# Layer 1's queries, keys and values as three fp16 products of high and low halves, and a new table of tick places

## The chip, the cores and the metric

The kernel runs on one core of one Trainium2 chip. TensorE (PE) multiplies, VectorE (DVE), ScalarE (ACT) and GpSimd (POOL) work on elements, SyncE (SP) issues every transfer. The metric is the device time of one execution in microseconds, the median of the runs.

## What is computed

Four layers follow one another on a batch of 32 sequences of 256 tokens and 256 channels. Layer 0 is a conditioned block of two normalisations over the whole sequence and two 256x256 products. Layer 1 is attention of 16 heads with a bias and a mask, and an MLP. Layer 2 is a stencil. Layer 3 is causal attention and an MLP with a gate. The change touches the first lines of layer 1:

```python
emb = jax.nn.silu(_sin_emb(timestep)) @ W_ada + b_ada
scale, shift = jnp.split(emb[:, None, :], 2, axis=-1)
x = _ln(src) * (1.0 + scale) + shift
q = (x @ Wq + bq).reshape(B, S, N_HEAD, HEAD_DIM).transpose(0, 2, 1, 3)
k = (x @ Wk + bk).reshape(B, S, N_HEAD, HEAD_DIM).transpose(0, 2, 1, 3)
v = (x @ Wv + bv).reshape(B, S, N_HEAD, HEAD_DIM).transpose(0, 2, 1, 3)
scores = jnp.einsum('bhqd,bhkd->bhqk', q / math.sqrt(HEAD_DIM), k)
```

## The kernel before

One program is written out for all 32 batches. Layers 0 to 2 of batch b begin at tick 64 b, layer 3 at tick 64 b + 160, so that layer 1 of one batch runs beside layer 3 of one two or three batches earlier. Every piece of work has a name and a place (the tables `P`, `LATE`, `OWN`, `SPLIT`, and `place`); `OWN` holds the places of the first two batches (0, 1) and of the last two (-2, -1). For each engine the ticks are walked in order and the pieces due at a tick are written in the order in which the loop names them. A tick therefore is not a time: it only sets the order of pieces on one engine. Each engine works its list strictly in that order, and waits on semaphores where it needs another engine (`Lane.wait_ge`). SP has such a list too, of transfers.

The pieces around the change, in the order of the data of a batch:

- DVE `n1_*` and `n2_*`: the two normalisations of layer 0 (statistics L874 to L878, sum L883 to L885, `all_center` L890, `all_scale` L895 and L899, `all_gate` L903); PE's `n1_ones` (L1513) and `n2_ones` (L1531) spread the sums, POOL's `n1_rstd` and `n2_rstd` (L531, L533) make the reciprocal roots; PE's `win` and `wout` are the two products (`lin_T` L1332, `lin_N` L1395).
- POOL's `xb` (L574) adds a row of `rows` to X, DVE's `x1` adds the product and takes statistics (L909, L912), ACT's `x1_norm` and POOL's `ada` (L582, L584) normalise and modulate.
- PE's `t1` turns X into bank F (L1402), ACT's `t1_out` copies it to H1 (L1226). PE's `q1`, `k1` (L1332) and `v1` (L1395) multiply H1 by the weights in Wf in fp32. ACT's `q1_out` and `k1_out` add the bias (L1179) and write a rounded copy (L1194), POOL's `q1_lo` and `k1_lo` the remainder (L547, L550), DVE's `v1_out` fills VW (L1009).
- SP's `stack` (L475, L479) moves QU, QH, KU, KH into the stacks Qs and Ks. PE's `score` (L1426), DVE's `bias` (L931), ACT's `exp` (L1153), PE's `flip` (L1436), the copies `ev0` and `ev1` (L1158, L938), PE's `pv` (L1451) and `ct` (L1461) are a unit of attention: two heads; 8 units a batch and layer.
- Layer 3 makes the same three products from fp16 halves already: ACT's `t3_out` writes the high half HB (L1256), DVE's `t3_lo` the low half (`rest`, L870), PE's `split_T` (L1344) and `split_N` (L1357) make three products for each fp32 one from WS_p3. The MLPs' first products are made so as well; their weights are split once, at the start (`split_scale` L800 and others).
- `warm` and `keep` put filler matmuls (L1293) on PE at the places and in the numbers of the table `WARM`.

Of the kernel before, what the change touches and what calls it, by code (L numbers as in the profile page):

```python
# [48 lines left out]
def begin(layer, b):  # L49
# [15 lines left out]
    "s_pm": 67, "s_b": 68, "s_r": 75, "s_rp": 80, "s_re": 95, "s_ha": 81, "s_w": 98, "s_ab": 99, "s_row": 98,  # L65
    "s_mm": 102, "s_f": 101, "ld_w1": -24, "ld_sten": -46, "ld_w3": -277, "coefs": -21, "split_w1": -8,
    "split_w1_hi": -4, "split_w1_lo": -2, "split_p3": 46, "split_p3_hi": 50, "split_p3_lo": 54, "split_w3": 82,
    "split_w3_hi": 88, "split_w3_lo": 92, "film_a": -72, "film": -62, "adas": -57, "scr": -48, "m3": -58,
# [127 lines left out]
def build(nc, A, OUT, scr, NB=32):  # L196
# [11 lines left out]
    def at(t, piece):  # L208
        return due[piece].get(t, [])
# [1513 lines left out]
```

## Time and profile before

| what | us |
|---|---|
| median of 3 runs | 2625.06 (2623.78 to 2630.91) |
| the profiled execution | 2623.82 |
| its span, first to last instruction | 2622.5 |
| mean granted TensorE clock over the span | 0.993 |

| engine | busy us | share of the span |
|---|---|---|
| PE, matmuls | 2511.0 | 96% |
| PE, weight loads | 2045.2 | 78% |
| DVE | 2000.5 | 76% |
| ACT | 2104.4 | 80% |
| POOL | 1525.1 | 58% |

Matmuls are pipelined and overlap in the records, so the duration of one (0.273 us for an fp16 one of 256 columns) is not what it costs: the distance from one start to the next is. A matmul of fp32 stands as two records. Idle time is counted from 150 ns on.

### The profile page before, as it was taken

Reading aid. Unit: us, or ns where it says so; the run is one execution under the profiler, and the core shown is the slowest. Engines: PE = TensorE matmul, PEld = TensorE weight load, DVE = VectorE, ACT = ScalarE, POOL = GpSimd, SP = SyncE. Lnnn points to the kernel's source line nnn. Section 1 sums busy time; section 2 is a strip of 40 time slices with the busy share of each in tenths; the row PEclk is TensorE's granted clock in tenths of the full one; section 3 lists DMA queues with packets and bytes.
Section 4 is the critical chain, followed back from the end, with each engine's and each line's share of the span. In section 5 each row is a group of like instructions: output and inputs, shape, how many; then the busy total and the mean of one; then the engine's idle time right before and its main releaser. Section 6 shows DMA issues by size and latency. Waiting matters only on the chain.

```text
span 2622.5 us, 57389 instructions
## 1 busy us (share of the span) xinstructions
PE 2511.0 (96%) x18897; PEld 2045.2 (78%) x18897; DVE 2000.5 (76%) x7326; ACT 2104.4 (80%) x4691; POOL 1525.1 (58%) x1486
## 2 busy tenths in 40 slices
PE   7888999999999999999999999999999999999988
PEld 6666788887878888788788788787777788877776
DVE  6777787778887777888777787877788877778653
ACT  1557888888888888888888888988888888888775
POOL 3566666555666655656665565675556666555421
PEclk8899999999999999999999999999999999999999
DMA  5444344433344443334443333444333344333311
GB/s 207 122 131 114 99 118 127 120 109 97 97 113 120 125 114 113 91 97 121 123 123 112 102 104 97 121 125 119 108 103 94 110 121 127 116 103 96 84 29 33
DMA packets 178103, 287.64 MB, mean 110 GB/s; under 512 B 46032, under 2 KB 99280, under 8 KB 177424
## 3 DMA queue, kind: packets, MB, share of 16 engines
q1 hardware_dynamic: 177808, 283.97, 37.4%
q8 instruction: 153, 2.51, 0.4%
q14 instruction: 142, 1.16, 0.2%
HBM read 174.64 MB, written 8.45 MB: 70 GB/s over the span
## 4 chain that ended last, share of the span: by engine, by line
PE 48%; POOL 19%; DVE 12%; ACT 10%; issue 5%; SPq 3%; DMA 2%; POOLq 0%; DVEq 0%; ACTq 0%
PE bank L1413 12%; POOL BT L562 9%; PE bank L1344 7%; PE bank L1436 6%; PE bank L1395 5%; PE bank L1332 5%; PE bank L1451 4%; PE bank L1426 4%; DVE PB L931 3%; PE bank L1402 2%; PE bank L1584 2%; SPq L479 2%; ACT AA L1179 2%; ACT PB L1153 2%; POOL KU L550 1%
## 5 line engine op out<-in xcount | busy, mean ns | idle before, releaser
L1153 ACT ACTIVATE PB<-PB,mx 128x256 f32<-128x256 f32 (+1 forms) x2048 | 823.6, 473 | 38.1 <-DVE mx L931 36.9
L562 POOL TENSOR_TENSOR BT<-BT,MN 128x1024 f32<-128x1024 f32 x256 | 545.7, 2144 | 78.0 <-DMA BT<-in_bias 77.7
L1436 PE MATMUL bank<-ident,PB 128*128 128x128 f32 x3584 | 498.6, 274 | 5.6 <-ACT PT L1158 2.6
L1436 PEld LDWEIGHTS bank<-ident,PB 128*128 128x128 f32 x3584 | 426.8, 141 | 68.7 <-issue 11.5
L1426 PE MATMUL bank<-Ks,Qs 96*128 96x512 f32 (+1 forms) x1024 | 401.4, 445 | 20.9 <-DVE mx L931 10.1
L931 DVE CUSTOM_DVE_ANT_0 PB<-bank,BT 128x256 f32<-128x256 f32 x1024 | 372.4, 419 | 53.2 <-PE bank L1426 50.8
L1344 PE MATMUL bank<-TN,WS_w 128*128 128x256 f16 x3072 | 378.6, 273 | 31.2 <-ACT AA L1179 14.9
L931 DVE CUSTOM_DVE_ANT_0 PB<-bank,caus 128x128 f32<-128x128 f32 (+1 forms) x1024 | 310.8, 350 | 96.4 <-PE bank L1426 95.3
L938 DVE COPY PT<-bank 128x512 f32<-128x512 f32 (+1 forms) x512 | 316.8, 619 | 69.9 <-PE bank L1436 69.8
L1344 PEld LDWEIGHTS bank<-TN,WS_w 128*128 128x128 f16 x3072 | 282.6, 98 | 105.6 <-ACT AA L1179 29.1
L1158 ACT ACTIVATE PT<-bank 128x512 f32<-128x512 f32 (+1 forms) x512 | 272.7, 533 | 48.8 <-PE bank L1436 43.3
L1451 PE MATMUL bank<-PT,VW 128*32 128x256 f32 (+1 forms) x4096 | 249.5, 361 | 2.1 <-DVE PT L938 1.1
L1413 PE MATMUL bank<-Wf,BB 128*128 128x256 f32 x1024 | 243.2, 381 | 5.6 <-ACT BB L1168 5.5
L1413 PE MATMUL bank<-Wf,AA 128*128 128x256 f32 x1024 | 234.6, 381 | 2.5 <-ACT AA L1247 2.5
L547 POOL TENSOR_TENSOR QU<-QU,QH 128x512 fp32r<-128x512 f32 x64 | 82.4, 1287 | 250.6 <-ACT QH L1194 250.6
L1426 PEld LDWEIGHTS bank<-Ks,Qs 96*128 96x128 f32 x1024 | 177.0, 191 | 55.8 <-DVE mx L931 24.6
L1413 PEld LDWEIGHTS bank<-Wf,BB 128*128 128x128 f32 x1024 | 187.2, 190 | 38.0 <-issue 16.1
L1413 PEld LDWEIGHTS bank<-Wf,AA 128*128 128x128 f32 x1024 | 191.3, 190 | 31.9 <-issue 3.6
L1451 PEld LDWEIGHTS bank<-PT,VW 128*32 128x32 f32 x4096 | 108.2, 109 | 96.7 <-issue 47.4
L1164 ACT ACTIVATE ET<-bank 128x256 f32<-128x256 f32 x256 | 96.5, 377 | 100.4 <-PE bank L1451 98.0
L931 DVE DVE_READ_ACCUMULATOR2_ANT mx<- 128x1 f32 x2048 | 168.6, 82 | 0.0
L537 POOL TENSOR_SCALAR smx<-smx 128x2 f32<-128x2 f32 x32 | 7.6, 236 | 267.4 <-DVE smx L912 267.4
(250 smaller groups left out, 4790.9 us busy)
## 6 DMA issues: line engine op xcount, KB each, us to landing
BT<-in_bias SPq DMA_DIRECT2D x256, 512.0 KB, 4.7
Qs<-QH SPq DMA_DIRECT2D x512, 64.0 KB, 2.4
Ks<-KH SPq DMA_DIRECT2D x1024, 32.0 KB, 2.0
Qs<-QU SPq DMA_DIRECT2D x256, 64.0 KB, 2.5
Ks<-KU SPq DMA_DIRECT2D x512, 32.0 KB, 2.0
XT<-in_xT SPq DMA_DIRECT2D x32, 256.0 KB, 2.8
X<-in_x SPq DMA_DIRECT2D x32, 256.0 KB, 2.9
AB<-ada_rows SPq DMA_DIRECT2D x32, 256.0 KB, 3.8
```

Source lines behind the costliest of these rows:

```text
L562: G.op.tensor_tensor(v2(BT[k % 4]), v2(BT[k % 4]), MN[:, :].unsqueeze(1).broadcast_to([128, 2, 512]), ALU.add).then_inc(g_bt, 1)
L931: V.op.tensor_tensor_reduce(PB[(2 * D + q) % 6][:, h * 256:h * 256 + w], bS[q][:, h * w:h * w + w], plus, -1.0, 3.0e38, ALU.add, ALU.min, ...
L938: V.op.tensor_copy(flipped(u.D, 1)[:, 0:w], bP[1][:, 0:w]).then_inc(v_ev, 1)
L1153: S.op.activation(o, o, ACT.Exp, scale=-1.0, bias=mx[u.layer][:, c:c + 1]).then_inc(a_exp, 1)
L1158: S.op.activation(flipped(u.D, 0)[:, 0:w], bP[0][:, 0:w], ACT.Copy).then_inc(a_ev, 1)
L1332: last = T.op.matmul(half(ps, m), Wf[:, a + k * 256 + m * 128:a + k * 256 + m * 128 + 128], half(x, k), start=(k == 0), stop=(k == 1))
L1344: last = T.op.matmul(half(ps, m), w, v[:, k * 256:k * 256 + 256], start=(k == 0 and i == 0), stop=(k == 1 and i == 2))
L1395: last = T.op.matmul(half(ps, m), x[:, k * 256 + m * 128:k * 256 + m * 128 + 128], Wf[:, a + k * 256:a + k * 256 + 256], start=(k == 0), s ...
L1413: last = T.op.matmul(half(ps, q), x[:, f * 256 + q * 128:f * 256 + q * 128 + 128], Wf[:, c:c + 256], start=(g == 0 and f == 0 and q == 0), ...
L1426: T.op.matmul(bS[q][:, 0:2 * w].rearrange("p (h k) -> p h k", h=2), Qs[i][0:96, et * 256 + q * 128:et * 256 + q * 128 + 128], k2[:, :, 0:w ...
L1436: last = T.op.transpose(bP[h][:, c * 128:c * 128 + 128], PB[(2 * u.D + q) % 6][:, h * 256 + k * 128:h * 256 + k * 128 + 128], ident[:, :])
L1451: last = T.op.matmul(half(bV, J % 2)[32 * s:32 * s + 32, q:256], VW[x][:, v:v + 32], flipped(u.D - 1 + et, h)[:, k * 256:k * 256 + 256 - q ...
```

## The change

Three things.

1. Layer 1's weights for q, k and v are loaded as fp32 into QU1, QH1 and KU1 at the start, scaled by factors found from their largest entries (`first_max`, `first_gains`, with two visits to PE, `first_turn` and `first_spread`, and one power on POOL), and split into a high and a low fp16 half in WP (`first_rest` and three activations on ACT). The factors are folded into the biases and into the ones of VW1.
2. ACT writes the high half of H1 with a scale, DVE the low half (`turned1`, piece `t1_lo`); `q1`, `k1`, `v1` become `split_T` and `split_N`.
3. Every entry of `P`, `OWN`, `SPLIT` and `WARM` is written anew.

```diff
-SQUARE = {n: 4096 + 512 * i for i, n in enumerate(("W_in", "W_out", "o1", "o3", "q1", "k1", "v1"))}
+SQUARE = {n: 4096 + 512 * i for i, n in enumerate(("W_in", "W_out", "o1", "o3"))}
+FIRST = {n: 10240 + 512 * i for i, n in enumerate(("q1", "k1", "v1"))}
...
 P = {
...
-    "t1": -22, "t1_out": -22, "x1_bo": -12, "q1": -19, "q1_out": -17, "q1_lo": -32, "k1": -15, "k1_out": -13,
-    "k1_lo": -28, "v1": -10, "v1_out": -9, "c1": 45, "c1_out": 44, "o1": 48, "m1": 51, "m1_rstd": 35, "m1_norm": 51,
...
+    "t1": -23, "t1_out": -24, "t1_lo": -21, "x1_bo": -18, "q1": -19, "q1_out": -17, "q1_lo": -27, "k1": -15,
+    "k1_out": -13, "k1_lo": -27, "v1": -12, "v1_out": -7, "c1": 46, "c1_out": 46, "o1": 48, "m1": 49, "m1_rstd": 30,
...
+    "split_p1": -55, "split_p1_hi": -50, "split_p1_lo": -45, "split_w1": -8, "split_w1_hi": -4, "split_w1_lo": -2,
...
 WARM = {
-    "start": 24, "c1": 12, "n1_ones_0": 8, "wout": 24, "t1_0": 13, "v1": 19, "flip": 1, "wout_1": 7, "n1_ones_2": 1,
-    "t3_0": 6, "n2_ones_3": 3, "v3": 15,
+    "start": 24, "c1": 12, "n1_ones_0": 2, "v1": 9, "win_1": 5, "w1_0": 3, "n2_ones_2": 1, "n1_ones_3": 4,
+    "v1_3": 1, "v3": 10,
 }
...
             square(d_wout, "W_out", "W_out")
+            for i, a in enumerate(FIRST.values()):
+                S.op.dma_start(raw1(i), A["wf"][:, a:a + 512]).then_inc(d_p1, 16)
             S.op.dma_start(rows[:, :], A["rows"].unsqueeze(0).broadcast_to([128, len(ROWS) * 256])).then_inc(d_rows, 16)
             S.op.dma_start(X[0][:, :], A["x"][0]).then_inc(d_xn[0], 16)
-            square(d_sq, "o1", "v1")
+            square(d_sq, "o1", "o3")
...
+                for b in at(t, "split_p1_hi"):
+                    if b == 0:
+                        G.wait_ge(v_p1, 14)
+                        G.op.tensor_tensor(wp[:, 13:14], wp[:, 8:9], mh[:, 0:1], ALU.pow).then_inc(g_p1, 1)
...
+            def first_max():
+
+                V.op.memset(ap[:, 11:12], 0.0).then_inc(v_p1, 1)
+                V.wait_ge(d_p1, 48)
+                for i, k in enumerate((0, 3, 10)):
+                    V.op.tensor_reduce(ap[:, k:k + 1], raw1(i), AX.X, ALU.max, apply_absolute_value=True).then_inc(v_p1, 1)
+                V.wait_ge(v_set, 48)
+                V.op.tensor_reduce(ap[0:32, 12:14], adar.rearrange("p (a n) -> p a n", a=2), AX.X, ALU.max,
+                                   apply_absolute_value=True).then_inc(v_p1, 1)
...
+            def first_gains():
+
+                ps = bP[1]
+                V.wait_ge(p_p1, 1)
+                V.op.tensor_reduce(ap[0:4, 14:15], ps[0:4, 0:128], AX.X, ALU.max).then_inc(v_p1, 1)
...
+                V.wait_ge(p_p1, 2)
+                V.op.tensor_scalar(wp[:, 0:4], ps[:, 128:132], 128.0, None, ALU.mult).then_inc(v_p1, 1)
...
+                V.wait_ge(g_p1, 1)
+                V.op.tensor_tensor(wp[:, 14:15], wp[:, 8:9], wp[:, 13:14], ALU.mult).then_inc(v_p1, 1)
...
+            def first_rest():
+
+                for i in range(3):
+                    V.wait_ge(a_p1, i + 1)
+                    V.op.scalar_tensor_tensor(out=first_lo(i), in0=raw1(i), scalar=wp[:, 10 + i:11 + i], in1=first_hi(i),
+                                              op0=ALU.mult, op1=ALU.subtract).then_inc(v_p1, 1)
...
+            def turned1(t):
+                for b in at(t, "t1_lo"):
+                    V.wait_ge(a_t1, b + 1)
+                    V.op.scalar_tensor_tensor(out=lo(H1), in0=bF[:, :], scalar=wp[:, 9:10], in1=hi(H1), op0=ALU.mult,
+                                              op1=ALU.subtract).then_inc(v_t1, 1)
...
                 for b in at(t, "t1_out"):
                     S.wait_ge(p_t1, b + 1)
                     S.wait_ge(p_v[1], b)
-                    S.op.activation(H1[:, :], bF[:, :], ACT.Copy).then_inc(a_t1, 1)
+                    S.wait_ge(v_p1, 15)
+                    S.op.activation(hi(H1), bF[:, :], ACT.Identity, scale=wp[:, 9:10]).then_inc(a_t1, 1)
...
                 def linear(ps, name, h):
-                    a = 512 * "qkv".index(name)
+                    W, k0, a = WP if x == 1 else WS["p3"], 1536, 512 * "qkv".index(name)
+                    if name == "v":
+                        return split_N(ps, W, k0, a, h)
+                    return split_T(ps, W, k0, lambda m, k: a + k * 256 + m * 128, h)
+
+                for b in at(t, f"q{x}"):
                     if x == 1:
-                        return lin_N(ps, "v1", h) if name == "v" else lin_T(ps, f"{name}1", h)
...
+                        T.wait_ge(v_p1, 29)
+                        T.wait_ge(v_t1, b + 1)
```

In `OWN[0]`, batch 0, the new pieces stand thus: on DVE `n1_gate` and `adas` -272, `split_p1` (`first_max`) -266, `n2_stats` -263, `n2_sum` -261, `split_p1_hi` (`first_gains`) -261, `n2_center` -254, `n2_scale` -231, `n2_gate` -225, `split_p1_lo` (`first_rest`) -205, `x1` -181, `t1_lo` -159; on POOL `n2_rstd` -378, `xb` -272 (before: -357, ahead of `n2_rstd` at -273), `split_p1_hi` -261; on PE `split_p1` -266, `n2_ones` -265, `split_p1_hi` -261, `wout` -218, `t1` -128. Among the other places of `P`: `stack` -4 becomes -8, `mask_add` -20 becomes -23, `ld_bt` -10 becomes -12, `mask` -28 becomes -34, `ld_xn` -80 becomes -37, `xb` -37 becomes -45.

## Rows read from the trace of the kernel before

**Rows 1.** The page, busy time of each engine, share of the span, instructions.

```profile
PE 2511.0 (96%) x18897; PEld 2045.2 (78%) x18897; DVE 2000.5 (76%) x7326; ACT 2104.4 (80%) x4691; POOL 1525.1 (58%) x1486
```

**Rows 2.** Busy time by stretches; columns named in its first line.

```profile
core 0: us, PE busy (x) PEld busy (x) DVE busy (x) ACT busy (x) POOL busy (x), PEclk, DMA share, GB/s
0.00:200.00 200.00, 161.14 (x1043) 131.29 (x1043) 141.87 (x453) 87.58 (x180) 99.11 (x97) 0.92 0.48 156
...
400.00:2300.00 1900.00, 1866.17 (x14221) 1525.42 (x14219) 1499.40 (x5510) 1609.31 (x3601) 1169.96 (x1131) 1.00 0.39 112
...
2420.00:2560.00 140.00, 128.44 (x998) 101.54 (x994) 84.91 (x332) 109.77 (x244) 52.93 (x53) 1.00 0.22 60
```

**Rows 3.** 400 to 2300: instructions on H, those on HB, writes of H.

```profile
400.00:2300.00 1900.00, 144.43 (x600) 108.18 (x600) 14.99 (x25) 1.00 0.39 112
...
400.00:2300.00 1900.00, 111.28 (x900) 81.91 (x900) 17.29 (x25) 14.95 (x25) 1.00 0.39 112
...
L1226 ACT ACTIVATE H<-bank x25: 597/599/601, 402.8 to 2251.7; 128x512 f32<-128x512 f32 x25
```

**Rows 4.** Chain of work within one batch: start us, us, what.

```profile
1106.44 1.29 POOL KU L550
...
1113.85 1.96 DMA Ks<-KU
1115.86 0.73 PE bank L1426 x2
```

**Rows 5.** PE in order of time: start us, us, line, out<-in, records.

```profile
1096.06 1.89 PE L1332 MATMUL bank<-H,Wf 128*128 128x256 f32 x8
1097.79 0.60 PE L1402 MATMUL bank<-ident,CX 128*128 128x128 f32 x4
...
1208.29 1.49 PE L1344 MATMUL bank<-HB,WS_p 128*128 128x256 f16 x12
1209.53 0.71 PE L1426 MATMUL bank<-Ks,Qs 96*128 96x512 f32 x2
```

**Rows 6.** Groups, 400 to 2300: busy us, mean ns | idle us before, releaser.

```profile
L1179 ACT ACTIVATE QU<-bank,cols,ws 128x256 f32<-128x256 f32 x50 | 25.0, 549 | 0.0
L1179 ACT ACTIVATE QU<-bank,cols 128x256 f32<-128x256 f32 x50 | 20.5, 460 | 0.0
...
L895 DVE SCALAR_TENSOR_TENSOR bank<-bank,sm,bT 128x512 f32<-128x512 f32 x49 | 36.8, 751 | 0.5 <-POOL sm L533 0.5
...
L870 DVE TENSOR_TENSOR HB<-bank,HB 128x512 f16<-128x512 f32 x25 | 17.3, 691 | 61.3 <-ACT HB L1256 61.3
```

**Rows 7.** All engines in the start, batch 0, in order of time.

```profile
21.34 1.27 POOL L574 TENSOR_TENSOR X<-X,rows 128x512 f32<-128x512 f32 x1 [0.83 <-DMA X<-in_x]
...
32.47 0.69 DVE L874 BATCH_NORM_STATS2 sm<-XT 128x6 f32<-128x512 f32 x1 [2.12 <-ACT XT L1179]
...
34.56 0.75 DVE L890 SCALAR_TENSOR_TENSOR bank<-XT,sm,gT 128x512 f32<-128x512 f32 x1
...
34.73 0.62 POOL L531 TENSOR_SCALAR sm<-sm 128x1 f32<-128x1 f32 x1 [12.12 <-DVE sm L885]
...
39.23 3.40 PE L1395 MATMUL bank<-Wf,FU 128*128 128x256 f32 x8 [5.10 <-DVE FU L903]
...
44.28 2.43 DVE L800 TENSOR_REDUCE am<-BB 128x1 f32<-128x512 f32 x4
...
50.91 3.07 PE L1293 MATMUL bank<-ones,ident 128*128 128x128 f32 x26
...
51.11 0.60 ACT L1226 ACTIVATE H<-bank 128x512 f32<-128x512 f32 x1 [3.95 <-PE bank L1402]
...
53.81 1.89 PE L1332 MATMUL bank<-H,Wf 128*128 128x256 f32 x8
```

**Rows 8.** Stretches of the start, columns as in rows 2.

```profile
39.20:42.60 3.40, 3.37 (x10) 2.78 (x11) 0.00 (x0) 0.00 (x0) 0.00 (x0) 0.57 1.07 396
42.60:50.40 7.80, 5.50 (x50) 5.20 (x48) 7.52 (x18) 1.09 (x2) 4.38 (x6) 1.00 0.86 352
```

More of the change, by code:

```diff
@@ L55 @@
 P = {
-    "score0": -1, "score1": -1, "bias0": 0, "bias1": 0, "exp0": 2, "exp1": 2, "flip0": 8, "flip1": 8, "ev0": 8,
-    "ev1": 9, "pv": 14, "cx": 14, "ct": 17, "pvn": 19, "ld_bt": -10, "mask_add": -20, "stack": -4, "ld_x": -85,
-    "ld_xn": -80, "ld_ab": -77, "ld_mask": -76, "mask": -28, "n1_stats": -80, "n1_ones": -69, "n1_sum": -61,
[6 rows of a table removed]
[L65 to L68, printed above, removed]
[4 rows of a table removed]
+    "score0": -1, "score1": -1, "bias0": 0, "bias1": 0, "exp0": 1, "exp1": 2, "flip0": 8, "flip1": 8, "ev0": 7,
+    "ev1": 9, "pv": 14, "cx": 13, "ct": 17, "pvn": 17, "ld_bt": -12, "mask_add": -23, "stack": -8, "ld_x": -78,
+    "ld_xn": -37, "ld_ab": -36, "ld_mask": -117, "mask": -34, "n1_stats": -75, "n1_ones": -69, "n1_sum": -69,
[6 rows of a table added]
+    "f1": 74, "s_pm": 63, "s_b": 67, "s_r": 75, "s_rp": 82, "s_re": 96, "s_ha": 81, "s_w": 97, "s_ab": 97,
+    "s_row": 98, "s_mm": 103, "s_f": 103, "ld_w1": -24, "ld_sten": -46, "ld_w3": -277, "coefs": -21,
[6 rows of a table added]
+    "out": 74, "st_out": 71,
 }
@@ L789, in row_moves @@
                     V.op.tensor_tensor(Gm[:, c:c + 1], Gm[:, c:c + 1], ident[:, e:e + 1], ALU.add).then_inc(v_mv, 1)
+            def first_max():
[6 more added lines that the diff above has]
+                                   apply_absolute_value=True).then_inc(v_p1, 1)
+                V.wait_ge(v_p1, 3)
+                V.op.scalar_tensor_tensor(out=ap[:, 0:6], in0=ap[:, 0:6], scalar=-1.0, in1=ap[:, 0:6], op0=ALU.mult,
+                                          op1=ALU.max).then_inc(v_p1, 1)
+                V.wait_ge(v_p1, 5)
+                V.op.tensor_tensor(ap[0:32, 11:12], ap[0:32, 12:13], ap[0:32, 13:14], ALU.add).then_inc(v_p1, 1)
+                V.wait_ge(v_p1, 6)
+                V.op.tensor_reduce(ap[:, 8:10], ap[:, 0:6].rearrange("p (a n) -> p a n", a=2), AX.X, ALU.max).then_inc(v_p1, 1)
@@ new lines, in first_rest @@
+            def first_rest():
[3 more added lines that the diff above has]
+                                              op0=ALU.mult, op1=ALU.subtract).then_inc(v_p1, 1)
+                V.wait_ge(d_rows, 16)
+                V.wait_ge(g_zero, 6)
+                V.wait_ge(v_p1, 22)
+                bv = rows[:, ROWS["bv1"] * 256:ROWS["bv1"] * 256 + 256]
+                one = VW[1][:, :].rearrange("p (h c) -> p h c", c=32)[:, :, 16:32]
+                for v, k in ((cols[:, COLS["bq1"][0]:COLS["bq1"][1]], 15), (cols[:, COLS["bk1"][0]:COLS["bk1"][1]], 16),
+                             (bv, 17), (one, 17)):
+                    V.op.tensor_scalar(v, v, wp[:, k:k + 1], None, ALU.mult).then_inc(v_p1, 1)
@@ L848, in split_rest @@
                     V.wait_ge(d_rows, 16)
-                    V.op.scalar_tensor_tensor(out=bq, in0=ps[:, 256:258], scalar=0.25, in1=bq, op0=ALU.mult, op1=ALU.add).then_inc(v_ws, 1)
+                    V.op.tensor_tensor(bq, ps[:, 256:258], bq, ALU.add).then_inc(v_ws, 1)
                     V.op.tensor_tensor(bk, ps[:, 258:260], bk, ALU.add).then_inc(v_ws, 1)
@@ L1113, in vector @@
                 front(t)
+                turned1(t)
                 values(t, 1)
@@ L1123, in vector @@
                         row_moves()
+                for b in at(t, "split_p1"):
+                    if b == 0:
+                        first_max()
+                for b in at(t, "split_p1_hi"):
+                    if b == 0:
+                        first_gains()
+                for b in at(t, "split_p1_lo"):
+                    if b == 0:
+                        first_rest()
                 for n in ORDER:
@@ L1181, in project @@
             def project(t, x):
[L1182 removed]
+                for n, U, hi, p, a in (("q", QU[x], QH[x], p_q[x], a_q[x]), ("k", KU[x], KH[x], p_k[x], a_k[x])):
                     for b in at(t, f"{n}{x}_out"):
@@ L1205, in scalar @@
                 attention(t)
+                for b in at(t, "split_p1_lo"):
+                    if b == 0:
+                        S.wait_ge(v_p1, 22)
+                        for i in range(3):
+                            S.op.activation(first_hi(i), raw1(i), ACT.Identity, scale=wp[:, 10 + i:11 + i]).then_inc(a_p1, 1)
                 for n in ORDER:
@@ L1358, in split_N, with first_turn, first_spread @@
                 return last
+            def first_turn():
+                T.wait_ge(v_p1, 8)
+                T.op.transpose(bP[1][0:4, 0:128], ap[:, 8:12], ident[:, :]).then_inc(p_p1, 1)
+            def first_spread():
+                T.wait_ge(v_p1, 11)
+                T.op.matmul(bP[1][:, 128:132], ones[0:4, :], ap[0:4, 0:4], start=True, stop=True).then_inc(p_p1, 1)
             def split_max(n):
@@ L1499, in tensor @@
                 attention(t)
+                for b in at(t, "split_p1"):
+                    if b == 0:
+                        first_turn()
+                for b in at(t, "split_p1_hi"):
+                    if b == 0:
+                        first_spread()
                 for n in ORDER:
```

83 lines of the change are left out of this document (50 added, 33 removed), and 130 rows, old and new, of tables (OWN, P).

## The prediction

> **What bounds the kernel now.** I read the busy table first: TensorE (PE) is busy 2511.0 of 2622.5 us, ScalarE (ACT) 2104.4, VectorE (DVE) 2000.5, GpSimd (POOL) 1525.1 [rows 1]. An average says little of a kernel with a start and an end, so next the table by stretches: in the 1900 us from 400 to 2300 PE is busy 1866.17 us, 98.2%, at full clock, while ACT has 1609.31 (85%), DVE 1499.40 (79%), POOL 1169.96 (62%) [rows 2]. In the first 200 us PE is busy only 161 us, at a mean granted clock of 0.92, and from 2420 to 2560 it is busy 128.44 of 140 [rows 2]. So there are three regimes: a start set by a chain of dependent steps through all engines, a long middle set by PE, an end between the two. In the middle ACT writes H, once a batch, 25 times from 402.8 to 2251.7: (2251.7 - 402.8)/24 = 77.0 us a batch [rows 3]. PE's idle time there is 1900 - 1866.17 = 33.8 us, 1.4 us a batch.
>
> Busy is not the same as full speed, so I also followed the chain of work within one batch. Mostly it runs from matmul group to matmul group. But after the layer-1 queries and keys it leaves PE: the remainder of KU on POOL at 1106.44, the stack's transfer at 1113.85, and the scores at 1115.86 that wait for it [rows 4]. That chain is a neighbour of exactly the work that changes, and PE fills it with other work rather than standing still.
>
> **Part 1: the products of layer 1, the only large term.** `lin_T` and `lin_N` make 12 fp32 matmuls of 256 columns a batch for q, k and v; the trace holds two records for each, 24 in all. Eight of them start at 1096.06 and the next group at 1097.79: 1.73 us, 0.216 us a record, so 24 x 0.216 = 5.19 us a batch [rows 5]. The changed kernel makes 36 fp16 products of the same 256 columns, by the helper that layer 3 uses already. Its price is in the trace: 12 products on HB start at 1208.29 and the next group at 1209.53, 1.24 us, so 36 cost 3.72 us [rows 5]. The saving is 1.47 us a batch by starts. By PE's busy time over the 1900 us, 25 batches of each, it is (144.43 - 111.28)/25 = 1.33 us [rows 3]. I take 1.40, and keep both. The weight loads don't bind: 900 loads of fp16 are busy 81.91 us under 111.28 us of matmul [rows 3].
>
> Whether loads are hidden matters, since the change turns 24 of them into 36. The row of the 12 products shows them hidden: 12 starts in 1.24 us leave no room for 12 loads of 0.091 us (81.91/900) beside 12 streams [rows 3, 5]. The Trainium skill ("TensorE: Matmul & The Clock Gate", Part 3, The mechanism) has a sentence by which loads overlap running matmuls only when their row group differs, and these all use the whole array. By it a batch would cost 24 x (0.180 + 0.216) before and 36 x (0.091 + 0.103) after, 2.5 us less instead of 1.4, and the kernel would come near 2560; this case's trace disagrees in both forms, so it gets no chance.
>
> Over 32 batches 1.40 is 44.8 us (42.6 to 47.0). Only batches that run while PE is full give it to the end time. Batches 0 to 2 have their front before 190 us, where PE waits for the chain anyway [rows 2], so I count 29: 40.6 us (38.6 to 42.6).
>
> **Part 2: the remainder of H1 on DVE.** New is `t1_lo`: one scalar-tensor-tensor on 128x512 out of PSUM, per batch. The nearest row is L895, 0.75 us; layer 3's plain one took 0.69 [rows 6]. 32 x 0.75 = 24 us on an engine with 400 us idle in the middle [rows 2]. ACT's write of H becomes fp16 with a pointer scale: a pointer scale costs ACT 549 - 460 = 89 ns on 256 columns [rows 6]; at most 0.2 us a batch on an engine with 15% idle. The work that hides both is PE's attention and MLP work between `t1` and `q1`: three ticks before, four now. What DVE may lose beside is a wait: in layer 3 DVE stands 61.3 us in 25 batches, 2.45 us each, before this same step, because ACT writes HB late [rows 6]. Queued behind it on DVE are the bias additions (L931) for which ACT's exponentials and then PE's flips wait. PE does not visibly pay for it in layer 3: it is 98% busy there. So between 0 and 2.45 us a batch; nearest to the layer-3 row seen from PE, near 0. Of the saving I let 10% come back through this and through the chain from keys to scores [rows 4], where one step of 0.75 us is added and two products of 0.49 us less are taken away: +4 us (0 to +20).
>
> **Part 3: the start.** Weights: the three raw blocks (768 KB) are loaded into QU1, QH1 and KU1 ahead of `rows`, X[0] and the rest, the same bytes as before. `rows` is needed by `xb`, which ran at 21.34 [rows 7]; it now may land some 3 us later, still before its new place, so 0.
>
> `first_max` follows the ada rows on DVE (done at 32.47 - 2.12 = 30.35): three maxima over 128x512 at 2.43/4 = 0.61, one over 32x512 the same, four small ones at 0.2: about 3.2 us, until 33.6; `n2_stats` started at 32.47, so +1.1 us [rows 7]. `first_gains` is dearer, because it sits on DVE between `n2_sum` and `n2_center` and waits for others: two visits to PE and one power on POOL. On POOL this power is queued behind `n2_rstd` (two steps, the first 0.62, from 34.73) and now `xb` (1.27), which was done long before [rows 7]. From `n2_sum` at about 35.9: POOL is through at 35.9 + 1.2 + 1.3 + 0.6 = 39.0, DVE's last six small steps take 1.2, and `n2_center` starts near 40.3 instead of 34.56; `n2_scale` behind it waited for POOL before (two steps from 34.73 on, to 36.0) and need not now: it moves from 36.0 to 40.3 + 0.8 = 41.1. That is +5.1 us on the chain of batch 0. `first_rest` (three remainders, four scalings, 3.5 us) lies on DVE while PE makes `wout` (39.23 to 42.6) [rows 7]: 0.
>
> Against it stand the fillers. Of 148 filler matmuls the new table keeps 71. The 13 after `t1` ran from 50.91 to 53.81 while H was ready at 51.11 + 0.60 = 51.7 [rows 7]: 2.1 us of pure delay goes. `t1_lo` adds 0.8, and q, k, v give 0.43 to 0.49 each. The 16 fillers before flips and the 10 at `v1`, 2.9/13 = 0.22 us each, may give up to 5 us more. The counterweight is the clock. Rows first: from 39.2 to 42.6, after 5.1 us in which PE waited, the mean granted clock was 0.57 (mostly the level of 1.2 GHz) and `wout` took 3.40 us for 8 records; from 42.6 on, with the 48 filler records in it, it was 1.00 (2.4 GHz), and q took 1.89 [rows 7, 8]. Without the 24 fillers behind `wout` the 36 products of batch 0 may run at 1.2 GHz, twice 3.72: 3.7 us more. The Trainium skill ("TensorE: Matmul & The Clock Gate", Part 1) puts it as "the default state is throttled, and activity releases the throttle"; the rows agree, and it is the rule that speaks against this part of the change.
>
> Together: +5.1 - 2.1 + 0.8 - 1.4 = +2.4 with a warm clock, +6 to +7 with a cold one, down to -3 if the other fillers were on the path. I take +3 (-3 to +9).
>
> **Part 4: every tick place.** A tick is 77.0/64 = 1.2 us; a place changes the order only among pieces of the same engine. No row prices it. Bounds: it can win at most PE's idle time of the middle (34 us) and some of the start's (200 - 161 = 39 us) and of the end's (140 - 128 = 12 us) [rows 2], and in loss any of these again. The largest moves that I can read are harmless: `stack` earlier (-4 to -8), which gives the chain after the keys some 5 us more room; `mask_add` and `ld_bt` earlier; `mask` ahead of `q1_lo` on POOL. `ld_xn` goes from -80 to -37 on SP's queue, behind stacks of other units, with `xb` at -45 on POOL: if it binds, POOL stands still for a transfer, and the scores' bias behind it. I take 0, with +-12 in the range.
>
> **The sum.** The profiled execution took 2623.8 us (span 2622.5 and 1.3 around it); 2623.8 - 40.6 + 4 + 3 + 0 = 2590.2. The median of the runs stands 1.2 above the profiled one; I say 2591.
>
> **The rivals.**
> A, forecast: PE's saving passes almost whole: 2578 to 2605.
> B, more than whole: the new places also take out stalls. For it: in the middle 1.4 us a batch of idle time and, beside it, short stalls that the busy time hides; fewer fillers. If half the idle time goes too, 17 us: about 2572.
> C, no change: the middle is in truth set by the loop ACT-DVE-POOL around the step from keys to scores, and PE's time turns into waiting. For it: the chain does leave PE once a batch. Against: PE is 98.2% busy. It would give 2617 to 2633.
> D, slower: DVE's new wait. DVE stands before `t1_lo` until ACT has written H, as before HB, 2.45 us, plus 0.75 us of work; in this stretch the bias additions queue behind it, and PE's flips with them. If all of it reaches PE: 3.2 - 1.4 = 1.8 us a batch lost, 29 x 1.8 = 52, 2680. It decides from 1.4 us a batch that reach PE; at two thirds, 2.1 us, it is 2625 + 20 + 3 = 2648. Against it: layer 3 carries the same wait.
> E: the change does not do what it says, fp16 products in layer 1 at another rate than in layer 3. Same shapes and helper: I give it 1 in 100 and leave it out of the rest.
>
> **How the numbers follow.** A 0.65, B 0.17, C 0.09, D 0.09 (E in it). The time is A's, 2591. The range: A reaches 2578 to 2605; down to the middle of B, 2568, and up to where A with both costly bounds (4 to 20, 3 to 9) ends, 2591 + 16 + 6 = 2613. Faster by over 0.3% (below 2617; 0.3% is about what a measurement of this kernel can tell from none) is A, B and a little of C: 0.86; within: the rest of C and a little of D: 0.07; slower: 0.07.
>
> **What would show it.** In the trace after: 1152 fp16 records on H with WP, 12 in about 1.24 us, and no fp32 record on H; a batch every 75.6 us in the middle against 77.0; PE still over 97% busy from 400 to 2300; DVE's `t1_lo` 0.75 us; `n2_center` of batch 0 near 40 instead of 34.56; first write of H 3 to 5 us later than 51.11; clock below 1 in q, k, v of batch 0. Wrong is the prediction if the period stays above 76.4 with PE idle more (C, D; D if DVE's wait for H is over 2 us and PE waits for flips), or if the start costs over 10 us.

## The result, and the profile after

The changed kernel takes 2605.3 us (median of 4 runs) where the kernel before takes 2624.4 in the same sitting: ratio 0.9926, 95% interval 0.9912 to 0.994. It is 19 us faster; I had forecast 34. One execution of the experiment `warm_start` took 8635.8 us, in the slow state, and is left out of its numbers; all others are in the fast state. The page of the changed kernel, busy times and shares of the chain that ended last; under them the same share line of the page of before, which I had not put among my rows:

```profile
PE 2470.5 (95%) x19148; PEld 2005.6 (77%) x19148; DVE 2043.6 (78%) x7387; ACT 2115.3 (81%) x4694; POOL 1536.1 (59%) x1487
...
PE 69%; DVE 15%; SPq 4%; ACT 4%; issue 3%; POOL 2%; DMA 2%; DVEq 0%; POOLq 0%; ACTq 0%
```

```profile
PE 48%; POOL 19%; DVE 12%; ACT 10%; issue 5%; SPq 3%; DMA 2%; POOLq 0%; DVEq 0%; ACTq 0%
```

The stretches of [rows 2] after the change (same columns):

```profile
0.00:200.00 200.00, 150.20 (x908) 119.20 (x909) 150.99 (x462) 85.37 (x174) 90.63 (x92) 0.81 0.46 146
400.00:2300.00 1900.00, 1865.78 (x14728) 1523.18 (x14727) 1547.34 (x5641) 1645.17 (x3661) 1193.27 (x1154) 1.00 0.40 113
2420.00:2560.00 140.00, 121.06 (x938) 96.62 (x940) 82.65 (x321) 101.03 (x228) 47.60 (x53) 1.00 0.19 46
```

In the middle PE is as full as before, though it has less to do in each batch: more batches pass in the same 1900 us. The instructions on H in that stretch, as in [rows 3], and one group of 12 products with its neighbour, as in [rows 5]:

```profile
L1447 PE MATMUL bank<-H,WP x600: 272/273/283, 411.1 to 2235.5; 128*128 128x256 f16 x150
L1459 PE MATMUL bank<-WP,H x300: 272/273/283, 419.2 to 2238.2; 128*128 128x256 f16 x150
L1330 ACT ACTIVATE H<-bank,wp x25: 687/687/689, 408.9 to 2226.7; 128x512 f16<-128x512 f32 x25
```

```profile
1098.36 1.48 PE L1447 MATMUL bank<-H,WP 128*128 128x256 f16 x12
1099.60 0.60 PE L1538 MATMUL bank<-Ks,Qs 96*128 96x256 f32 x2
```

12 products take 1.24 us, as forecast. H is written every (2226.7 - 408.9)/24 = 75.74 us; by [rows 3] it was 77.04. The two kernels compare in three pieces, cut at the 6th and the 30th write of H (402.8 and 2251.7 before):

| piece | before | after | difference |
|---|---|---|---|
| start to the 6th write | 402.8 | 408.9 | +6.1 |
| 24 batches | 1848.9 | 1817.8 | -31.1 |
| 30th write to the span's end | 370.8 | 377.0 | +6.2 |
| span | 2622.5 | 2603.7 | -18.8 |

So 1.30 us a batch is won in the middle, and in these two traces 12.3 us are given back at the ends. The three pieces are not equally firm. Five kernels with the same middle, the changed one and four of the experiments, have periods of 75.73 to 75.79. But seven whose lists are the same up to the 6th write reach it at 403.6 to 409.2, and nine that have the new places from tick 1850 on take 377.0 to 384.5 us after the 30th. By these spreads the start costs 0.8 to 6.4 us and the end 6 to 14; of the kernel before there is one trace. The runs had to tell what the 1.30 is made of and where the ends lose.

### The profile page after: what moved, and what is told of

It reads as the page before. It is cut to its first block, busy times and chain, and to the rows that moved or that the text cites. A ratio compares the mean times of both kernels' runs of the same rounds, so it can differ in the third digit from the quotient of the medians.

```text
span 2603.7 us, 57961 instructions
## 1 busy us (share of the span) xinstructions
PE 2470.5 (95%) x19148; PEld 2005.6 (77%) x19148; DVE 2043.6 (78%) x7387; ACT 2115.3 (81%) x4694; POOL 1536.1 (59%) x1487
## 4 chain that ended last, share of the span: by engine, by line
PE 69%; DVE 15%; SPq 4%; ACT 4%; issue 3%; POOL 2%; DMA 2%; DVEq 0%; POOLq 0%; ACTq 0%
PE bank L1525 17%; PE bank L1447 12%; PE bank L1548 10%; PE bank L1538 6%; PE bank L1563 6%; PE bank L1507 6%; DVE PB L1010 4%; PE bank L1514 3%; SPq L496 3%; PE bank L1459 3%; PE bank L1701 2%; DVE bank L969 2%; PE bank L1436 2%; SPq L492 1%; DMA Ks<-KU 1%
## 5 line engine op out<-in xcount | busy, mean ns | idle before, releaser
L579 POOL TENSOR_TENSOR BT<-BT,MN 128x1024 f32<-128x1024 f32 x256 | 556.9, 2180 | 122.5 <-DMA BT<-in_bias 121.0
L1548 PE MATMUL bank<-ident,PB 128*128 128x128 f32 x3584 | 486.4, 274 | 11.5 <-ACT PT L1254 5.5
L1548 PEld LDWEIGHTS bank<-ident,PB 128*128 128x128 f32 x3584 | 421.6, 141 | 63.4 <-ACT PB L1249 10.6
L1538 PE MATMUL bank<-Ks,Qs 96*128 96x512 f32 (+1 forms) x1024 | 364.6, 430 | 25.5 <-DMA Ks<-KU 12.0
L1525 PE MATMUL bank<-Wf,BB 128*128 128x256 f32 x1024 | 236.8, 379 | 0.8 <-ACT BB L1264 0.6
L1538 PEld LDWEIGHTS bank<-Ks,Qs 96*128 96x128 f32 x1024 | 168.1, 192 | 67.7 <-DVE mx L1010 22.3
L554 POOL TENSOR_SCALAR smm<-smm 128x2 f32<-128x2 f32 x32 | 7.2, 226 | 280.0 <-DVE smm L991 280.0
L1275 ACT ACTIVATE BB<-bank,cols 128x256 f32<-128x256 f32 x256 | 107.4, 470 | 44.3 <-PE bank L1447 44.3
```

The source lines that it names most:

```text
L579: G.op.tensor_tensor(v2(BT[k % 4]), v2(BT[k % 4]), MN[:, :].unsqueeze(1).broadcast_to([128, 2, 512]), ALU.add).then_inc(g_bt, 1)
L1275: S.op.activation(half(out, m), half(ps, m), ACT.Identity, scale=scale(m), bias=bias(m)).then_inc(sem, 1)
L1525: last = T.op.matmul(half(ps, q), x[:, f * 256 + q * 128:f * 256 + q * 128 + 128], Wf[:, c:c + 256], start=(g == 0 and f == 0 and q == 0), ...
L1538: T.op.matmul(bS[q][:, 0:2 * w].rearrange("p (h k) -> p h k", h=2), Qs[i][0:96, et * 256 + q * 128:et * 256 + q * 128 + 128], k2[:, :, 0:w ...
L1548: last = T.op.transpose(bP[h][:, c * 128:c * 128 + 128], PB[(2 * u.D + q) % 6][:, h * 256 + k * 128:h * 256 + k * 128 + 128], ident[:, :])
```

## Experiments

All were timed in five rounds; the kernel before took 2623.9 to 2627.4 beside them. A period is the mean gap between the 6th and the 30th write of H, as above. The wanted comparison is between orders, so several kernels hold two tables of places: ticks below a bound use one table, later ticks the other.

### The places alone

```diff
 # the kernel before: lin_T and lin_N in fp32, H by ACT alone
-P, OWN, SPLIT, WARM of before
+P, OWN, SPLIT, WARM of the change
```

> The fp32 products of before with every new tick place and the new filler table; nothing is split, so the pieces t1_lo and split_p1 do not exist. Theory P (the saving comes from the products, the places bring nothing by themselves): within 6 us of before, a batch every 77 us in the middle. Theory T (the new places are the gain, and they were needed for it): 10 us or more faster than before, a batch every 76.5 us or less. If the new places only suit the new arithmetic, it is slower than before by 10 us or more.

2625.3 us, ratio 0.9999 (0.9988 to 1.0011). Its 6th write of H is at 402.9, its 30th at 2244.3, its span 2622.7: nothing at the start, a period of 76.73 instead of 77.04 (-7.5 us), and 378.4 instead of 370.8 us from the 30th write to the end (+7.6). New places alone are worth nothing in sum, as theory P had it; the 0.31 that they win in the middle is lost at the end.

### The products alone, in the old order

```diff
 # the changed kernel
+OLD_P, OLD_OWN, OLD_SPLIT = tables of before, with "t1_lo": -20
 def place(piece, b, NB, layer="", base=0):
+    ticks 330 to 1850: old place; outside: new place
```

> The changed kernel, with the old tick places between tick 330 and tick 1850 (about batch 5 to batch 28 of layer 1; t1_lo two ticks after t1_out), the new ones before and after. Changed: a batch every 75.8 us there. Theory P: the period stays within 0.2 us of 75.8, so within 5 us of the changed kernel. Theory T: at least 0.5 us a batch more, 12 us or more over the changed kernel.

2642.0 us, ratio 1.0063 (1.0045 to 1.008). The middle of this kernel, and its writes of H:

```profile
400.00:2300.00 1900.00, 1846.01 (x14470) 1493.25 (x14469) 1512.56 (x5532) 1607.78 (x3594) 1162.18 (x1132) 1.00 0.40 112
...
L1419 ACT ACTIVATE H<-bank,wp x25: 687/687/687, 409.2 to 2261.3; 128x512 f16<-128x512 f32 x25
```

The period is 77.17: the same products that PE does faster bring nothing, and PE is busy 20 us less than before in the same 1900 us [rows 2]. The saving has turned into waiting. That is what rival C of the prediction would do, here in the old order. What holds the old order?

Among PE's waits are two that come in every batch and that the kernel before has not. The larger is for the new step `t1_lo` (`DVE H`; waits of PE, 400 to 2300: us in total, times, longest):

```profile
PE bank L1536 <- DVE H L1174: 10.8, 24, 0.5
```

### One step of POOL moved: the mask MN

```diff
 # mid_old, OLD_P
-    "mask": -28
+    "mask": -34
```

> mid_old with one tick place changed: POOL makes the mask MN at -34 instead of -28, so that it no longer stands between QU and KU. Theory X (a period is a stretch from H's write to the batch's first score, set by the chain keys, ACT, POOL, stack, score, and a rest set by PE; in the old order the chain is the longer in the first stretch): in mid_old the subtraction KU starts at 1114.23 behind MN (1.50 us) although KH was ready at about 1113.0, so KU, the stack and the score come 1.2 us earlier in each batch; the period falls from 77.1 to about 75.9 in ticks 330 to 1850 (about 24 batches), the time from 2642 to about 2613 (2608 to 2625), and PE's busy time in a batch stays. Rival P (the middle is set by PE's order and its other waits, MN is under cover): the period stays 77.1 and the time 2640 to 2644.

2638.1 us, ratio 1.0049 (1.0037 to 1.0061); period 76.98. I had expected a gain of 1.2 us a batch from taking MN out from between QU and KU; it is 0.19, next to rival P. But the trace became regular: 21 of the 24 gaps are 76.8 or 76.9, as if one loop held them, a circle of steps that leads from one batch into the next. Its chain of work, start us, us, what (cut):

```profile
1049.42 0.28 DVE sm L1053
...
1049.78 0.20 POOL sm L637
...
1055.66 6.29 POOL BT L668 x3
...
1070.70 2.09 POOL BT L668
1072.78 0.19 POOL smt L643
...
1074.34 1.10 ACT BB L1358 x2
...
1076.53 0.61 ACT TN L1462
...
1084.98 1.01 DVE FU L1067 x2
...
1090.39 1.97 PE bank L1614 x8
```

In 24.5 of the 76.8 us POOL works back to back, from the n1 rstd at 1049.78 to the last step on smt. POOL had stood idle right before this, and it was DVE's `n1_sum` that it waited for (POOL in order of time; idle us and releaser in brackets):

```profile
1049.78 0.19 POOL L637 TENSOR_SCALAR sm<-sm 128x1 f32<-128x1 f32 x1 [7.07 <-DVE sm L1053]
```

The kernel before has the same: in 400 to 2300 POOL waited for the sums of its two normalisations 178.8 us in 48 times, and between the 6th and the 30th write its chain goes over the steps on smt in 17 of 24 batches (in 24 of 24 in mid_mask, in none in the changed kernel).

```profile
POOL sm L531 <- DVE sm L885: 178.8, 48, 7.8
```

An engine that is busy 62% of the time can set the period: it stands 7 us in front of one step and then has 24.5 us of queued work on which the next normalisation hangs.

This loop is not only POOL, though. Between `t1` and the next product of an MLP (on TN; L1344 before, L1536 here) it passes the stretch in which q, k and v are made. There the two kernels differ. First the chain of the kernel before, then that of mid_mask (start us, us, what):

```profile
1402.40 0.59 PE bank L1402 x4
...
1404.09 1.73 PE bank L1332 x8
...
1416.90 1.43 PE bank L1344 x12
```

```profile
1101.40 0.60 PE bank L1603 x4
...
1102.03 0.70 ACT H L1419
...
1103.41 0.41 DVE PB L1099
...
1111.22 0.73 ACT KU L1364 x2
...
1115.98 1.43 PE bank L1536 x12
```

Before, the chain stays on PE there, with q, k and v on it. In mid_mask it leaves PE for the write of H, `t1_lo` and the bias additions behind it on DVE, and then for ACT's exponentials and evictions. By PE's starts the stretch is 14.51 us long before and 14.58 in all five kernels with the old places and the new products, though PE has 1.47 us less to do in it. With the new places it falls from 15.81 (ticks_only) to 14.62 us (the changed kernel): there 1.19 of the 1.47 comes through. This is where the saving goes in the old order: the loop is as long as before because the branch over DVE and ACT takes PE's place. The part of `t1_lo` in that branch can be estimated from the rows: it and the longer write of H add 0.67 + 0.10 us to it, about half of what is missing. No run moved `t1_lo` alone (I had put it one tick ahead of `q1` in the old table; the new one has two), so how much a better place would have freed is open.

### All of POOL's steps moved

```diff
 # mid_old, OLD_P: the 20 places of POOL as in the change
-    "q1_lo": -32, "k1_lo": -28, "mask": -28, "mask_add": -20, "m4_rstd": 44, "m1_b": 48, ...
+    "q1_lo": -27, "k1_lo": -27, "mask": -34, "mask_add": -23, "m4_rstd": 40, "m1_b": 56, ...
```

> mid_old with the 20 places of POOL's own steps in ticks 330 to 1850 as in the change, all other places old. Theory L (in the old order a loop through POOL's queue sets the period at 76.8 whatever PE has to do: POOL stands at the n1 rstd, then works 24.5 us back to back up to smt, which ACT, DVE and in the end PE wait for; the chain of the run mid_mask shows it, 23% of it on POOL, 32% on PE): with POOL's steps in the new order the loop is shorter, PE's saving shows, the period is 75.4 to 76.2, the time 2604 to 2622, and PE's share of the chain is 55% or more. Rival M (the loop is closed by DVE's and ACT's places as well, POOL's are not enough): period 76.6 to 77.1, time 2632 to 2642.

2684.8 us, ratio 1.0225 (1.0206 to 1.0243): slower by 2%, where I had expected the loop to shorten. The writes of H and the chain's shares:

```profile
L1419 ACT ACTIVATE H<-bank,wp x24: 687/687/687, 408.8 to 2225.1; 128x512 f16<-128x512 f32 x24
```

```profile
PE 31%; POOL 24%; DVE 16%; ACT 15%; issue 7%; SPq 3%; DMA 2%; DVEq 0%; POOLq 0%; ACTq 0%
```

The period is (2225.1 - 408.8)/23 = 78.97, 2.0 above mid_mask. Seven additions to BT (2.1 us each) now lie between the n1 rstd and smt instead of six: the POOL stretch of the chain goes from 24.5 to 26.6 us. I had expected the opposite, and 20 places moved at once, so it is luck that the outcome tells something: by the trace the one thing that changed in the POOL stretch is an addition of 2.1 us more, and 20 of 24 gaps are 78.9, 2.1 above the 76.8 of mid_mask, with PE's work unchanged.

### Only smt moved

```diff
 # mid_old, OLD_P
-    "m4_rstd": 44
+    "m4_rstd": 40
```

> mid_old with a single place changed: m4_rstd, the four short POOL instructions on smt, at 40 instead of 44, so that they stand ahead of one addition to the bias tile BT (2.14 us) and more. Theory L with the position of smt as the deciding link: the period falls by 0.7 to 1.5 us, the time by 17 to 36 us to 2606 to 2625. If other links of POOL's queue are as late (BT, KU of layer 1 behind MN): under 0.4 us a batch, 2632 to 2642.

2640.4 us, ratio 1.0059 (1.0039 to 1.0079); period 77.21. No effect. In mid_old and here MN still stands before KU, and between the 6th and the 30th write the chain runs over KU and the stack in 13 batches and over smt in 11 (mid_old: 11 and 12): two loops of nearly the same length, and shortening one shows nothing.

### `n1_sum` earlier on DVE, beside the mask

```diff
 # mid_mask, OLD_P
-    "n1_sum": -61
+    "n1_sum": -69
```

> mid_mask with one more place changed in ticks 330 to 1850: DVE's n1_sum at -69 (as in the change) instead of -61. In mid_mask the period is 76.8 in nearly every batch and its chain runs from DVE's n1_sum (1049.42) over POOL's n1 rstd, for which POOL has stood 7.07 us, through 24.5 us of POOL back to back up to smt, on to ACT, DVE's n2 work and PE; mid_pool, with one addition to BT (2.1 us) more between the two, had a period of 78.9, 2.1 longer. Theory L (this loop sets the old order's period): with n1_sum 8 ticks earlier POOL isn't held there, its queue runs up to 7 us earlier, the loop is no longer the longest, and PE's saving shows: period 75.4 to 76.0 and time 2605 to 2622, PE's share of the chain 55% or more. Rival (another loop of nearly the same length stands behind it, or DVE waits in front of n1_sum for PE's n1_ones): period 76.4 to 77.0, time 2632 to 2640.

2631.4 us, ratio 1.0023 (1.0009 to 1.0038); 12 runs. Period 76.75, 18 of 24 gaps 76.5 or 76.6. The chain's shares:

```profile
PE 58%; DVE 15%; ACT 14%; issue 6%; SPq 2%; POOL 2%; DMA 2%; DVEq 0%; POOLq 0%; ACTq 0%
```

POOL has left the chain, as theory L said, and PE's share has almost doubled from 32%. The time followed by 0.2 to 0.3 us a batch, not by 1: behind the POOL loop stands another at 76.5. Its chain goes over the write of H and `t1_lo` again, then over ACT's in-order queue, where the layer-1 evictions and the norm of AA stand behind exponentials, and later over DVE's n2 steps (start us, us, what):

```profile
1103.91 1.38 ACT PB L1338 x4
1105.29 0.73 ACT KU L1364 x2
...
1106.58 1.08 ACT AA L1358 x2
...
1111.50 0.85 ACT AA L1364 x2
```

The rival of this run won.

### The mask back between QU and KU, in the new order

```diff
 # the changed kernel, P
-    "mask": -34, "k1_lo": -27
+    "mask": -26, "k1_lo": -26
```

> The changed kernel with the mask MN at -26 and KU's subtraction k1_lo at -26 instead of -34 and -27: MN (1.50 us) again stands between QU and KU in all batches without a place of their own (2 to 29). Theory X: KU starts up to 1.5 us later; in the changed kernel the stretch from H's write to the first score has PE busy 20.38 of 21.26 us, so little slack takes it up; the period rises by 0.8 to 1.5 us, the time by 22 to 42 us to 2627 to 2647. Rival P (MN's place costs nothing): 2604 to 2607.

2646.7 us, ratio 1.0083 (1.0068 to 1.0098), 41 us above the changed kernel; period 77.30, +1.56 for a step of 1.50 us. That is a mean of uneven gaps: the shortest went from 75.4 to 76.4, the longest is 80.0. The wait on PE that answers for it, 400 to 2300 (the changed kernel has 2.2 us in 5 times):

```profile
PE bank L1538 <- DMA Ks<-KU: 32.8, 24, 2.9
```

The chain of [rows 4] has no slack in the new order. In the old order the same move was worth 0.19.

### One product of three left out

```diff
 # the changed kernel, layer 1 only
 for i, (w, v) in enumerate(((h, hi(x)), (h, lo(x)), (l, hi(x)))):
+    if two and i == 1:
+        continue
```

> The changed kernel without the product of H's low half in layer 1's queries, keys and values: 12 fewer matmuls and weight loads a batch, some 1.24 us of PE (1.48 us for 12 records that overlap), 24 of the 36 remain. It leaves out that part of the result. Theory X: q and k (8 of the 12) lie in the stretch from H's write to the first score, v may lie in either; PE is busy 20.38 of 21.26 us there, so the chain (QU and KU on POOL, then the stack) takes part of the gain: the period falls by 0.3 to 0.9 us, the time by 8 to 26 us to 2579 to 2597. Theory P (PE's work passes through one for one): 1.24 us in each of 31 batches, 38 us, 2565 to 2570.

2602.3 us, ratio 0.9916 (0.9903 to 0.9928), 3 us below the changed kernel for 31 x 1.24 = 38 us less work on PE. The period is 75.60 (-0.14), and waits have appeared on PE that the changed kernel has not (400 to 2300):

```profile
PE bank L1463 <- ACT KU L1275: 8.3, 25, 0.3
...
PE bank L1518 <- ACT AA L1269: 6.2, 25, 0.2
```

So the new order has a floor as well, at 75.3 (10 of this kernel's 24 gaps), 1.5 below the old one's 76.8; the changed kernel stands almost on it.

### The end in the old order

```diff
 # the changed kernel
 def place(...):
+    from tick 1850 on: old place, with t1_lo at -20 to -23
```

> The changed kernel with the old tick places from tick 1850 on (the last three batches). From the write of H of batch 30 to the end the changed kernel takes 299 us, the kernel before took 294. Theory E (the new places of the end cost 5 us): 4 to 7 us faster than the changed kernel. Rival (the added step on VectorE costs at the end, whatever the places): within 2 us of the changed kernel.

2601.5 us, ratio 0.9907 (0.9887 to 0.9927), 4 us below the changed kernel by medians, with intervals that overlap. In the profiled executions the piece from the 30th write of H (2225.8) to the end of the span (2595.2) is 369.4 us instead of 377.0: 7.6 less, the same 7.6 by which ticks_only was longer than before. Its profiled execution was the fastest of its six. Against the nine kernels with the new places there (377.0 to 384.5 us) the 369.4 and the 370.8 of the kernel before stand apart, and ticks_only, without the new products, took 378.4: the loss at the end belongs to the new places there, not to the products. By the times only about half of it can be seen.

### The start: the gains of batch 0 later

```diff
 # the changed kernel, OWN[0]
-    "x1": -181, "x1_rstd": -181, "split_p1_hi": -261, "split_p1_lo": -205
+    "x1": -199, "x1_rstd": -200, "split_p1_hi": -198, "split_p1_lo": -196
```

> The changed kernel with the gains and the remainders of the layer-1 weights moved behind x1 of batch 0, out of the second normalisation: the centring of that normalisation started at 39.45 us against 34.56 before. Theory S (the start is a chain, and what is added to it is added to the time): centring of batch 0 at 35.7 us, first write of H 3.5 to 4 us earlier than 55.7, the whole 3 to 5 us faster than the changed kernel. Rival (later waits take it up): under 1.5 us.

2613.0 us, ratio 0.995 (0.9932 to 0.9968), 7.6 above the changed kernel. n2_center came at 35.97 and x1 at 44.46, as expected. But the maxima of `split_w1` then ran on DVE at 54.34, and PE, which has their turn queued ahead of `t1`, stood for them (PE in order of time):

```profile
57.63 0.37 PE L1476 MATMUL bank<-ident,am 128*1 128x128 f32 x1 [10.23 <-DVE am L888]
...
57.80 1.06 PE L1514 MATMUL bank<-ident,X 128*128 128x128 f32 x4
```

H was written at 58.90. That explains part of the loss only: of the 10.6 us by which this trace is longer than the changed kernel's, 3.2 lie ahead of the 6th write (412.1) and 7.6 behind the 30th, where both kernels have the same places; what made the end longer was not looked into. The next kernel moved that turn behind the first products:

```diff
 # gains_late, OWN[0]
-    "split_w1": -168
+    "split_w1": -118
```

> The changed kernel with batch 0's gains behind n2_center as in gains_late, and PE's turn of split_w1's maxima moved from tick -168 behind the first products (-118), so that it doesn't stand in front of t1 on PE. If the order on PE was what undid gains_late: n2_center at about 36.0, wout at 40.7, x1 at 44.5, t1 at about 51.5, H's first write at 52 to 53 instead of 55.7, and the time 3 to 4 us below that of the changed kernel (2600 to 2603). If H's write is bound by DVE's order (gains, first_rest and split_w1's maxima all ahead of something that t1 needs), no gain or a loss as in gains_late (2606 to 2613).

2610.1 us, ratio 0.9944 (0.9932 to 0.9956). H was written at 52.1, as expected, yet PE's products began only at 56.00, after 3.95 us in front of `t1_lo`: DVE had `first_rest` and batch 1's n1 statistics ahead of it.

```profile
55.11 0.74 DVE L1085 SCALAR_TENSOR_TENSOR H<-bank,wp,H 128x512 f16<-128x512 f32 x1
55.77 2.45 DVE L879 TENSOR_REDUCE am<-BB 128x1 f32<-128x512 f32 x4
...
56.00 2.72 PE L1447 MATMUL bank<-H,WP 128*128 128x256 f16 x12 [3.95 <-DVE H L1085]
```

The maxima of `split_w1`, now behind the first products, come later than in the changed kernel, where their turn on PE was at 52.22, and the 6th write of H is at 411.9, 3 us late; that the first is the cause of the second was not tried. In both kernels the DVE work that was pushed back came to stand in front of something else that PE needed.

### The start: a warm clock

```diff
 # the changed kernel, WARM
-    "v1": 9
+    "v1": 19, "wout": 24, "t1_0": 8
```

> The changed kernel with more idle transposes on PE in batch 0: 24 ahead of wout, 8 ahead of t1 and 19 instead of 9 ahead of v1, to raise the granted clock before q, k and v of batch 0, which took 2.72 to 2.74 us for 12 products each against 1.24 us in batch 15. If the clock is what lengthens them and it follows what PE did before: q, k and v at 1.3 to 1.7 us, granted clock in 50 to 60 us 0.9 or more, the first batches 2 to 4 us earlier, the time 2601 to 2604. If the first batches wait for DVE and not for PE: the products get faster and the time stays 2604 to 2607. If the extra transposes stand in the way: H later than 55.7 and the time 2606 to 2612.

2603.2 us, ratio 0.9906 (0.9888 to 0.9925), 2 below the changed kernel (5 by the ratios), which the intervals don't separate. First the changed kernel, a stretch (columns of [rows 2]) and its first products, then this one:

```profile
50.00:56.00 6.00, 1.49 (x5) 0.79 (x5) 3.13 (x10) 1.39 (x3) 3.39 (x5) 0.50 1.00 418
...
57.32 2.72 PE L1447 MATMUL bank<-H,WP 128*128 128x256 f16 x12 [1.66 <-DVE H L1085]
```

```profile
50.00:56.00 6.00, 4.72 (x42) 4.36 (x42) 3.15 (x11) 1.21 (x3) 3.81 (x3) 1.00 0.88 367
...
55.58 1.47 PE L1447 MATMUL bank<-H,WP 128*128 128x256 f16 x12
```

The clock did what was expected, 1.00 (2.4 GHz) after the fillers against 0.50 (1.2 GHz) after waiting, and 2.72 us became 1.47. What that is worth in the time is not shown: the 6th write of H came at 403.8 instead of 408.9, but mid_m4, without the added fillers, had it at 403.6; and 3.1 of the 5.1 us went again behind the 30th write (380.0 against 377.0), so the span is 1.8 us shorter.

## Why the prediction was right, and where it was not

**The middle: right in size, wrong in cause.** I forecast 1.40 us a batch less a tenth that comes back, 36.6 us over 29 batches, which is 30.3 over the 24 between the two writes; measured were 31.1. I took that for PE's saving passed through (rival A). The runs say it is not so: the products alone would have given -0.13 a batch, so it is luck that the size fits. The whole, 2605.3, lies at the upper edge of A. Four kernels hold the middle in all combinations:

| period, us | old places | new places |
|---|---|---|
| fp32 products | 77.04 | 76.73 |
| three fp16 products | 77.17 | 75.74 |

Neither half gives more than 0.31; together they give 1.30. In the old order the loops go over POOL, ACT and DVE, at 76.8 and 76.5, and in the stretch with q, k and v a branch over DVE and ACT takes 14.58 us where PE's work had taken 14.51, so faster products met it at once. The new order lowered the floor of the loops to about 75.3; with old products PE's work held it at 76.7 (73% of ticks_only's chain is PE). The period is the longest of several loops, and the change shortened two that were nearly equally long. That the second is lowered by the new places is shown by mid_old and two_new; which of the many places do it I could not settle: POOL's alone made it worse (mid_pool), `n1_sum` and `mask` together gave 0.4.

**Step that failed: "every tick place, 0".** The sum for the places alone is indeed 0, measured 2625.3, but they are what let the 1.40 through. I had argued that PE is busy 98.2%, and gave rival C 0.09 on that ground. A busy share of 98.2% bounds only what can be gained in the old order without taking PE's work away (34 us); it does not say what becomes of the work taken away. The page of before would have warned: 19% of its chain lies on POOL, 48% on PE. Rival C had the right outcome for the products alone, but not the loop: it named the step from keys to scores, and the one found goes over the normalisations, BT and smt.

**Part 1, the count of batches.** I let batches 3 to 31 pay. Only 24 of them lie in the piece that pays; the other 5, 6.3 us by my rate, lie in the pieces before the 6th and after the 30th write, where no gain is left to see. (Whether they gained and the ends lost more, or they gained nothing, the traces can't separate.)

**Part 2, `t1_lo`, and rival D.** DVE's step takes 0.742 us and DVE does not wait in front of it in the middle:

```profile
L1085 DVE SCALAR_TENSOR_TENSOR H<-bank,wp,H 128x512 f16<-128x512 f32 x25 | 18.5, 742 | 0.0
```

The four ticks between `t1` (-23) and `q1` (-19) cover it, and PE does not wait for it: rival D is false for the changed kernel. In the old order it was partly true: PE stood 10.8 us in 24 batches for `t1_lo`, and the chain went over it in 20 to 22 of 24 batches, which I had priced at near 0.

**Part 3, the start.** Forecast +3 (-3 to +9), measured +4.6 at the first write of H (55.70 against 51.11) and +6.1 at the sixth. Both are at the upper end of what kernels with the same start show: 52.66 to 55.70 at the first write and 403.6 to 409.2 (+0.8 to +6.4) at the sixth, so the +3 is not refuted. n2_center came at 39.45 (forecast 40.3), the remainders ran under `wout`, and q, k, v ran at half clock with 2.72 to 2.74 us for 12. The fillers that the change dropped had been holding the clock up: before, it was 1.00 from 42.6 to 50.4, with 48 filler records in it [rows 8], now 0.50 from 50 to 56. The Trainium skill ("TensorE: Matmul & The Clock Gate", Part 1) says that the throttled state is the default one and that activity ends it; these rows agree.

```profile
39.45 0.75 DVE L969 SCALAR_TENSOR_TENSOR bank<-XT,sm,gT 128x512 f32<-128x512 f32 x1
...
43.52 3.78 PE L1507 MATMUL bank<-Wf,FU 128*128 128x256 f32 x8 [6.18 <-DVE FU L982]
...
55.70 0.69 ACT L1330 ACTIVATE H<-bank,wp 128x512 f16<-128x512 f32 x1 [3.89 <-PE bank L1514]
```

**The end, not priced.** It costs 6.2 us in these traces, inside the +-12 that I had kept for the places. The new places there are the cause by the traces of ticks_only and end_old.

The terms add up: 2590.2 + 6.3 (batches) + 3.1 (start) + 6.2 (end) - 0.8 (middle) = 2605.0, the profiled execution's 2603.7 and 1.3 around it. This is bookkeeping of the two traces, which comes out by construction; it is no check of the causes.

## What to carry to other kernels

Before an engine's saved work is counted as saved time, read the chain's shares beside the busy shares: here an engine at 98% had only half of the chain, a loop over other engines was as long, and the saving turned into waiting. To find such a loop, look in the wait list for an in-order engine that stands long in front of one step with much queued behind it. Then compare, before and after, the stretch of the loop in which the saved work lies (14.51 and 14.58 us here): it shows which branch took over, and whether a step that the change itself added stands on it. Test a loop by putting a step of known length into it: 1.50 and 2.1 us of POOL gave 1.56 and 2.0 us a batch here, whereas taking one loop away gave 0.2, because the next was 0.3 behind. And before a few microseconds at the start or the end are explained from one trace, look how far traces with the same lists differ there: up to 7.5 us here. When faster work brings nothing in an old order, the order has to be set anew together with it, and judged together.

## What the runs showed of the hardware

- 12 fp16 matmuls of 128x128 by 128x256 with 12 weight loads of 98 ns each take 1.24 us from the first start to that of the next group at full clock (1.48 us in the profile), for H as moving and as stationary operand alike. In batch 0, after 4.92, 1.96 and 1.66 us in which PE waited and at granted clock 0.50, the profile gives 2.72 us.
- After 8 fp32 matmuls (`wout`, 3.78 us at 0.50) and a wait the clock was 0.50 in 50 to 56; with 24 filler matmuls (48 records) behind the same `wout` it was 1.00.
- POOL's multiplication of a 128x512 mask took 1.50 us and its addition to 128x1024 2.1 us: on an engine busy 61 to 62% of the middle (mid_mask, mask_late) each lengthened the period by about its own length when it stood in the loop.
